# GNN and FFN kernel: ScalarE shares the one-hots behind the last step, and SP issues most of the loads

## The reference, cut to what matters

```
time_feat = relu(edge_attr @ W_time.T + b_time)          # 212500 x 64
sums   = segment_sum(time_feat, src, num_segments=n)
counts = segment_sum(ones,      src, num_segments=n)
node_time_feat = sums / max(counts, 1)
fused = relu(concat([node_feat, node_time_feat]) @ W_fusion.T + b_fusion)
x = x + (layernorm(x) + fused @ W_up.T + b_up)
x = x + (y + shared_mlp(y) + top-2 of 4 experts(y)),  y = layernorm(x)
```

## Time and profile before

| | us |
|---|---|
| median of three runs | 2166.23 |
| the profiled execution, its own time | 2165.71 |
| its span, first to last instruction | 2163.9 |
| TensorE matmul busy | 2017.9 (93%) |
| VectorE busy | 1726.8 (80%) |
| ScalarE busy | 1312.9 (61%) |
| GpSimd busy | 1123.1 (52%) |

### The profile page before, as it was taken

One profiled execution on the slowest core, in us unless ns is written; L12 is line 12 of the kernel. 1 busy time (PEld: TensorE's weight loads), 2 busy tenths in 40 slices (PEclk: granted clock), 3 DMA queues, 4 the chain that ended last, 5 costly groups with the idle time before them and its releaser, 6 DMA issues.

```text
span 2163.9 us, 74888 instructions
## 1 busy us (share of the span) xinstructions
PE 2017.9 (93%) x26946; PEld 1674.7 (77%) x26946; DVE 1726.8 (80%) x5392; ACT 1312.9 (61%) x2811; POOL 1123.1 (52%) x915
## 2 busy tenths in 40 slices
PE   4788888999999899999999999699979999999998
PEld 1577676798888799999899999688856666666666
DVE  9888988888787899888678777599966767767675
ACT  2588778887888777778878777200024444444443
POOL 0587877878777888887878777300011111111110
PEclk7799999999999999999999999899989999999999
DMA  2244344676776677777678877577721211212110
GB/s 85 76 126 129 124 126 126 187 208 193 200 210 180 186 223 205 222 224 222 182 219 243 248 226 208 180 218 219 217 62 45 66 45 45 66 45 66 45 54 31
DMA packets 239406, 323.64 MB, mean 150 GB/s; under 512 B 42144, under 2 KB 213965, under 8 KB 238706
## 3 DMA queue, kind: packets, MB, share of 16 engines
q1 hardware_dynamic: 176564, 192.90, 33.6%
q0 software_dynamic: 41504, 103.41, 13.1%
q10 hardware_dynamic: 20970, 22.54, 3.7%
HBM read 186.34 MB, written 175.77 MB: 167 GB/s over the span
## 4 chain that ended last, share of the span: by engine, by line
PE 72%; DVE 9%; ACT 6%; DMA 6%; issue 5%; POOL 1%; SPq 1%; DVEq 0%; ACTq 0%; POOLq 0%
PE bank L747 16%; PE moved L718 13%; PE bank L848 10%; PE moved L861 7%; PE bank L704 6%; DMA table<-arena 5%; PE moved L747 4%; PE bank L722 3%; ACT arena L1686 2%; PE bank L888 2%; ACT arena L1680 2%; DVE arena L1394 2%; PE bank L731 1%; DVE arena L1178 1%; PE bank L666 1%
## 5 line engine op out<-in xcount | busy, mean ns | idle before, releaser
L1887 POOL DMA_INDIRECT table<-arena x832 | 1023.2, 1230 | 330.9 <-issue 262.6
L1686 ACT ACTIVATE arena<-moved 128x588 bf16<-128x588 f32 x832 | 546.5, 662 | 147.3 <-PE moved L718 108.2
L718 PE MATMUL moved<-arena 128*128 128x196 bf16 x4992 | 576.5, 251 | 8.4 <-ACT arena L1686 7.0
L718 PEld LDWEIGHTS moved<-arena 128*128 128x128 f16 x4992 | 444.4, 97 | 82.9 <-ACT arena L1686 21.0
L1680 ACT ACTIVATE arena<-bank 128x512 f32<-128x512 f32 x624 | 373.7, 599 | 145.2 <-PE bank L704 128.7
L1394 DVE TENSOR_TENSOR arena<-arena 128x2832 f16<-128x2832 f16 x208 | 338.3, 1627 | 17.1 <-PE moved L718 10.3
L747 PE MATMUL bank<-arena 128*128 128x64 bf16 (+1 forms) x7344 | 288.8, 194 | 18.9 <-DVE arena L1483 18.4
L747 PEld LDWEIGHTS bank<-arena 128*128 128x128 bf16 x7344 | 262.1, 98 | 30.0 <-DVE arena L1483 19.9
L1789 ACT ACTIVATE arena<-bank,w_all 128x512 f32<-128x512 f32 (+1 forms) x225 | 152.8, 679 | 207.0 <-PE bank L848 116.2
L1295 DVE TENSOR_TENSOR sums<-sums,bank 128x130 f32 x528 | 150.9, 286 | 153.8 <-PE bank L747 128.6
L1903 POOL TENSOR_TENSOR arena<-arena 128x4 f32<-128x4 f32 (+1 forms) x25 | 25.2, 1009 | 424.0 <-DVE arena L1591 424.0
(11 more groups left out here) (300 smaller groups left out, 3045.9 us busy)
## 6 DMA issues: line engine op xcount, KB each, us to landing
arena<-table SPq DMA_DIRECT2D x672, 147.0 KB, 2.9
arena<-in_attr SPq DMA_DIRECT2D x208, 144.0 KB
arena<-table ACTq DMA_DIRECT2D x144, 147.0 KB, 2.9
table<-arena POOLq DMA_INDIRECT x832
x_ln<-arena SPq DMA_DIRECT2D x98, 128.0 KB
arena<-in_x SPq DMA_DIRECT2D x97, 128.0 KB
arena<-x_ln SPq DMA_DIRECT2D x24, 512.0 KB, 4.7
out_rows<-arena SPq DMA_DIRECT2D x24, 512.0 KB, 3.2
```

The lines of the kernel that those rows point to most:

```text
L718: mm = e.matmul(moved8[:, 4 * (n % 2) + h, 0:PW], slot_all[s % NSLOT][:, t * SLOTS + h * RG:t * SLOTS + h * RG + P], upper(s, 0, PW)[:, t, ...
L1686: e.activation(row_buf[n % NROWS], moved8[:, 4 * (n % 2):4 * (n % 2) + 3, 0:PW], ACT.Copy).then_inc(s_rows, 1)
L1887: e.indirect_dma_start(out=table, out_offset=bass.IndirectOffsetOnAxis(ap=dest[s % NDEST][:, a:a + 1], axis=0), in_=row_buf[n % NROWS].rea ...
```

## The change

Of the third chunk of each load VectorE makes one block of the three (256 columns). ScalarE makes the other two: it copies the two numbers with their sign turned, takes the absolute value of `iota_lo` plus that (one instruction for a block), and writes relu(1 - that) for both blocks. TensorE waits for both engines at that chunk (`s_hot_more`). The two buffers for the absolute values lie in `row_buf`, which the scatters no longer use then; three small tiles are added in front of `row_buf` (20 bytes for each partition). SP issues all loads but every sixth (j % 6 == 5), which ScalarE issues four loads ahead of its own work. The three row numbers of a load are read by one register load, in all of the kernel's loads of the table.

```diff
+        low_turned = [carve([BLOCK - 1], f32) for _ in range(2)]
+        one_col = carve([1], f32)
+        off_by = [... row_buf[0:2], as [BLOCK - 1, NODES_A_BUCKET] ...]
...
-        def fetch_chunks(e, row_reg, t, buffer, landed):
+        def fetch_chunks(e, row_regs, t, buffer, landed):
+            e.reg_load(row_regs, load_rows[0:1, CL * t:CL * (t + 1)])
             for c in range(CL):
-                e.reg_load(row_reg, load_rows[0:1, CL * t + c:CL * t + c + 1])
-                row = e.snap(row_reg, min_val=0, max_val=CHUNKS * CH)
+                row = e.snap(row_regs[c], min_val=0, max_val=CHUNKS * CH)
                 e.dma_start(buffer[:, c, 0, :], table[bass.ds(row, CH), :]).then_inc(landed, 16)
...
@@ sync_program
-            for j in range(0, loads[LAST], 2):
-                load_behind(e, row_reg, j)
+            for j in range(loads[LAST]):
+                if j % 6 != 5:
+                    load_behind(e, row_regs, j)
@@ tensor_program, add_up_behind
                 e.wait_ge(s_hot, CL * BEHIND + i + 1)
+                if i % CL == CL - 1:
+                    e.wait_ge(s_hot_more, i // CL + 1)
@@ vector_program
+            e.memset(one_col, 1.0)
...
-                e.tensor_tensor(in_pairs(hot_chunk[i % len(hot_chunk)]), pairs(iota_lo, BLOCK), each_pair(lo_of, NODES_A_BUCKET), ALU.is_equal).then_inc(s_hot, 1)
+                made = 1 if i % CL == CL - 1 else BLOCK
+                e.tensor_tensor(in_pairs(hot_chunk[i % len(hot_chunk)][:, 0:made]), pairs(iota_lo, made), each_pair(lo_of[:, 0:made], NODES_A_BUCKET), ALU.is_equal).then_inc(s_hot, 1)
@@ scalar_program
-            for j in range(1, loads[LAST], 2):
-                load_behind(e, row_reg, j)
+            for j in range(loads[LAST]):
+                if j % 6 == 1 and j + 4 < loads[LAST]:
+                    load_behind(e, row_regs, j + 4)
+                i = CL * j + CL - 1
+                turned, off = low_turned[j % 2], off_by[j % 2]
+                e.wait_ge(behind_sem[j % len(behind_tab)], behind_landed(j))
+                if j >= 2:
+                    e.wait_ge(s_off, j - 1)
+                low = behind_tab[j % len(behind_tab)][:, CL - 1, 0, :].rearrange("p (h w) -> p h w", h=BLOCK)[:, 1:, LO]
+                e.activation(turned, low, ACT.Copy, scale=-1.0).then_inc(s_low_turned, 1)
+                e.wait_ge(s_low_turned, j + 1)
+                if j >= 2:
+                    e.wait_ge(s_hot_more, j - 1)
+                for h in range(1, BLOCK):
+                    ins = e.activation(off[:, h - 1, :], iota_lo, ACT.Abs, bias=turned[:, h - 1:h])
+                ins.then_inc(s_off, 1)
+                e.wait_ge(s_off, j + 1)
+                if i < len(hot_chunk):
+                    e.wait_ge(s_moved, NS * GS)
+                else:
+                    e.wait_ge(s_sum_ps, CL * BEHIND + i - len(hot_chunk) + 1)
+                e.activation(hot_chunk[i % len(hot_chunk)][:, 1:, :], off, ACT.Relu, scale=-1.0, bias=one_col).then_inc(s_hot_more, 1)
```

More of the change, by code:

```diff
@@ L107, in gnn_ffn @@
         s_table = [sem(f"s_table{i}") for i in range(NTB)]
+        s_low_turned, s_off, s_hot_more = sem("s_low_turned"), sem("s_off"), sem("s_hot_more")
         s_table_more = [sem(f"s_table_more{i}") for i in range(NPAY)]
@@ L276, in gnn_ffn @@
         iota_lo = carve([NODES_A_BUCKET], bf16)
+        off_by = [r.rearrange("p h w -> p (h w)")[:, 0:(BLOCK - 1) * NODES_A_BUCKET].rearrange("p (h c) -> p h c", h=BLOCK - 1) for r in row_buf[0:2]]
         shared_from = top[0]
@@ L554, in await_rows, with load_behind @@
                 e.wait_ge(s_scatter[g % NROWS], scattered(g))
-        def load_behind(e, row_reg, j):
+        def load_behind(e, row_regs, j):
             i = j % len(behind_tab)
@@ L563, in load_behind @@
                 e.wait_ge(s_moved, NS * GS)
-            fetch_chunks(e, row_reg, BEHIND + j, behind_tab[i], behind_sem[i])
+            fetch_chunks(e, row_regs, BEHIND + j, behind_tab[i], behind_sem[i])
         def behind_landed(j):
@@ L578, in load_attr @@
                 e.dma_start(attr_in[n % NATTR][0:ONES_AT], attr[:, n, :, :]).then_inc(s_attr[n % NATTR], 16)
-            row_reg = e.alloc_register("row")
+            row_regs = [e.alloc_register(f"row{c}") for c in range(CL)]
             def load_table(k, n):
@@ L590, in load_table @@
                     await_rows(e, k)
-                fetch_chunks(e, row_reg, t, tab[t % NTB], s_table[t % NTB])
+                fetch_chunks(e, row_regs, t, tab[t % NTB], s_table[t % NTB])
             for n in range(NATTR):
@@ L1777, in scalar_program @@
                     keep_rows(GS * (s - 1) + 3)
-            row_reg = e.alloc_register("row_odd")
+            row_regs = [e.alloc_register(f"row_other{c}") for c in range(CL)]
             e.wait_ge(s_size, size_no(LAST, "listed"))
```

## The result

The changed kernel takes 2171.98 us (median of 8 runs, 2167.10 to 2176.70); the kernel before, beside it on the same chip, 2164.54 (8 runs, 2157.85 to 2167.96). The ratio is 1.0037 [1.0023, 1.0052]: slower by 0.2 to 0.5%, where 2165.7 and no change were forecast. The time lies inside the stated range, and the third rival, SP starving a load, given a chance of 0.04, is what the profile shows.

The account below looks back on a forecast made before the run. The prediction took VectorE's queue, closing each load's loop through a register load, as the bound. Terms 0 x 96 - 0.1 - 0.1 + 0.06 = -0.1 us gave 2165.7 us; range for 8 in 10: 2159 to 2174.

Parts of the forecast that it names:

- the third rival: SP starves a load, VectorE waiting for landings: about 2180 us if five loads take SP above 12.6 us; chance 0.04.
- SP's queue: SP issuing five of six loads: about 1.8 us each, 9 us of 12.6, still early, so 0 us.
- the cover of 3.6 us: SP's room in six loads: five issued loads at 9 us against the 12.6 us VectorE needs for six.
- The start: VectorE's wait for load 0 and the first loads behind it: -0.1 us, bounds -0.6 and +0.5.
- VectorE's loop: VectorE's queue, first one-hot to next load's: closes through a register load, so the shorter third one-hot gains 0 us.
- ScalarE's share: ScalarE making two blocks a load: chain 1.76 us, with issues 1.96 against 2.105, so it costs nothing.
- the cover of 0.14: ScalarE's room a load: 1.96 us of work and issues against the pace of 2.105 us; called thin.
- TensorE's added wait: TensorE's extra wait at each load's third chunk: 0 us, with 0.13 us a chunk to spare.
- the first stretch: The earlier stretch, where SP's loads also lose two register loads of three beside the scatters: 0, bounds -3 to +3 us.

Follow-up runs that it names:

- The split alone: The kernel before with SP issuing five of six loads, ScalarE the sixth, each row number still by its own register load: 2179.79 us, 1.0072.
- the kernel with GpSimd: The changed kernel, ScalarE's blocks kept, with GpSimd issuing every third load, SP the other two and ScalarE none: 2163.40 us, 0.9999 against the kernel before.
- the moved register load: The kernel before with VectorE's register load of a column number moved from behind its add to behind the next one-hot: 2154.11 us, 0.9961.
- both other limits gone: The changed kernel with GpSimd issuing every third load, ScalarE none, and VectorE's register load behind the next one-hot: 2149.54 us, 0.993 against the kernel before.
- the run with the register load alone: The kernel before with one register load for a load's three row numbers, SP and ScalarE still issuing every other load: 2163.54 us, 0.9996.

## Why the prediction was wrong, point by point

**SP's queue: the step that failed.** The text said "A load will hold it about 1.8 us as above; five are 9 us of 6 x 2.105 = 12.6", and so 0 us. Of the 1.8, the three issues at 1.4 were right (1.38). The other 0.4 was for "its own register load and start", priced by a register load of one number, while the edit makes it load three: 0.668 us, and the gap is 0.88. (With one number the rows already had 1380.77 - 1378.30 - 1.98 = 0.49 there.) That gives 2.26 to 2.28. Left out altogether were the stalls at issue, 0.28 a load, although the row that was quoted has a maximum of 1407 ns; the text used them for ScalarE, as a reason for a slow outcome, and not for SP, to which the change moves most of the issues. Together 12.8 us for 12.6: of the cover of 3.6 us the register load and the gap took 5 x 0.48 = 2.4, the stalls 5 x 0.28 = 1.4. Neither alone would have used it up. The stalls could not simply be read off either: SP's were 7.5 us over 48 loads before, 0.16 a load, and why they grew to 0.28 stays open. The split alone (+16.6 us) and the kernel with GpSimd (level) show that what the edit gives SP to issue made the loss.

**The start: wrong for the same cause.** It was put at -0.1 us: load 2's last issue at +4.6 us from two loads of 1.8. Load 0 did land 1.7 us sooner, but with 2.26 to 2.30 a load and landing waits of 1.14, 1.95, 0.60 and 0.95 the first four loads lost 3.8. From the first issue to load 4's first one-hot 1390.41 - 1378.30 = 12.11 us became 1390.90 - 1376.68 = 14.22; with GpSimd's third it was 12.03. Of the 14.22, 9.11 are SP's four loads ahead of load 4; that load's last DMA then took 4.03 us to land, over the usual 3.0, and the reason for that isn't shown.

**The third rival had the mechanism and the price of a microsecond**, 16 us for each one by which five loads pass 12.6; the split alone, 0.9 over for 16.6, about bears that out. Its chance hung on the 9 us, so it fell with that term.

**VectorE's loop: right.** 0 us for a one-hot a third as long. Median 2.08 us before and after, 0.66 us from the second add's end, idle time in front of the first one-hot. The text expected 0.33 us of it, counted from the add's hand-over after 0.20; so counted 0.25 came (1443.07 + 0.20 to 1443.52; the 0.16 of the row counts from the add's end). The other 0.09 is that the short one-hot hands over to its add after its whole 0.29 us (1442.78 to 1443.07), not after 0.20. The run with GpSimd's third shows that the share gave nothing even with SP relieved, the moved register load shows why.

**ScalarE's share: its chain was right, its issue was not.** 1.79 us against 1.76, Abs 0.50 (0.51), Relu 0.72 (0.69). But issuing a load leaves 1.6 us beyond the Relu where 1.2 was put, by the same register load of three numbers: 2.07 us a load at the least and not 1.96, and the cover of 0.14 was nearly gone. TensorE never waited for it here, so it cost nothing that the profile shows; what it would cost with SP on time no run shows, as the run with GpSimd takes this issue away too. No table load stands among the groups of the stretch, as the Trainium skill, page "ScalarE: Activation LUTs", section "Table sets: the hidden batching unit", has it for copy, abs and relu. The rule of the Trainium skill's page "ScalarE: Activation LUTs", section "Rules for kernel authors", that relu and its like belong on VectorE, decided nothing here. Undoing the share gained nothing either, as SP set the pace, and with both other limits gone the share took the loop from 2.006 to 1.83 us.

**TensorE's added wait, the first stretch: right.** No wait of TensorE ends with ScalarE; the run with the register load alone, which has the first stretch's part of the change, is level.

## What to carry to other kernels

Work that is moved to another queue is to be priced on that queue with every instruction it brings, in the form it will have there and with the stalls that the row's maximum warns of, summed over its single issues. Here two terms that were each smaller than the cover used it up together. Ask first what closes the loop. Here a shorter instruction on the busiest engine gave nothing, one register load moved behind the next instruction gave 9 us, and only with that move did the shorter instruction shorten the loop.

## What the runs showed of the hardware

A register load's time grows with the numbers it reads: on SP 0.268 to 0.271 us (medians) for one, 0.662 to 0.696 for three, against 3 x 0.271 = 0.81 for three single ones. On ScalarE's queue the load of three takes 0.702, from its row in the changed kernel:

```profile
L551 ACTq TENSOR_LOAD <-load_rows x16: 693/702/889, 1381.2 to 1577.7; - x16
```

GpSimd takes 0.54 us for an issue where SP takes 0.33, from its row in the run that gave it a third of the loads:

```profile
L555 POOL DMA_DIRECT2D arena<-table x96: 536/536/592, 1380.0 to 1574.3; - x96
```

Some DMA issues hold SP or ScalarE 0.4 to 2.0 us instead of 0.33 (the longest, 2.03, in the run with the single register load alone): 36 of SP's 240 in the changed kernel, 15 of its 144 before. What holds these up stays open; no run tried it. GpSimd's 96 all last 0.54 to 0.59.
